# A stacked graph network on one core: the attention row s2 goes through memory, stored graph by graph and read back with step 1

## The reference, cut to what matters

```python
h = relu(layernorm(x))
for i in range(3):                        # the recurrent rounds
    aggr = einsum('bst,bsd->btd', adj != 0, h @ weight[i])
    h = gru_cell(aggr, h, w_ih, w_hh, b_ih, b_hh)     # gates r, z, n
x = x + h
h = relu(layernorm(x))
Wh = h @ W.T
s1, s2 = Wh @ a1, Wh @ a2                 # one value per node
e = leaky_relu(s1[:, :, None] + s2[:, None, :], 0.2)
att = softmax(where(adj == 0, -inf, e))
x = x + att @ Wh
```

## Time and profile before

| | before |
|---|---|
| time, median of 3 runs | 1824.64 us (1824.41 to 1824.9) |
| profiled execution | 1824.46 us, span 1822.6 us |
| PE busy | 1779.6 us (98%) |
| VectorE busy | 1417.3 us (78%) |
| ScalarE busy | 1022.5 us (56%) |
| POOL busy | 354.7 us (19%) |
| DMA, its queue's share | 30.0% of 16 engines |
| granted clock of TensorE, mean | 0.991 of full speed |

### The profile page before, as it was taken

The page is one execution under the profiler, slowest core; times in us unless marked ns, Lnnn a source line. Parts: engine busy times, 40 slices in busy tenths (PEclk is TensorE's granted clock), DMA queues, the critical chain, the costliest instruction groups (busy, mean ns, idle before and its releaser), DMA issues.

```text
span 1822.6 us, 32181 instructions
## 1 busy us (share of the span) xinstructions
PE 1779.6 (98%) x10492; PEld 945.1 (52%) x10492; DVE 1417.3 (78%) x2801; ACT 1022.5 (56%) x1822; POOL 354.7 (19%) x778
## 2 busy tenths in 40 slices
PE   6999999999999999999999999999999999999993
PEld 5444555545555454555545555454555545555552
DVE  6667788787887877788787887877788787887866
ACT  5556556555555555556555555555556555555552
POOL 1022130311303122130311303122130311303100
PEclk9999999999999999999999999999999999999997
DMA  3322332323323223322323324223322323323221
GB/s 104 76 64 65 70 75 58 90 66 69 87 40 104 57 59 91 69 75 58 89 66 68 87 39 105 57 60 90 69 75 58 88 67 68 88 39 88 41 69 41
DMA packets 325789, 128.87 MB, mean 71 GB/s; under 512 B 241280, under 2 KB 325760, under 8 KB 325760
## 3 DMA queue, kind: packets, MB, share of 16 engines
q1 hardware_dynamic: 325760, 128.50, 30.0%
HBM read 52.96 MB, written 16.78 MB: 38 GB/s over the span
## 4 chain that ended last, share of the span: by engine, by line
PE 96%; DVE 1%; issue 1%; ACT 0%; POOL 0%; DVEq 0%; POOLq 0%; ACTq 0%
PE z_bank L320 27%; PE r_bank L320 27%; PE hn_bank L320 14%; PE in_bank L320 14%; PE s_bank L320 3%; PE w_bank L320 3%; PE nb_bank L334 2%; PE nb_bank L335 2%; PE t_bank L762 2%; PE t_bank L776 1%; ACT relu_att L272 0%; DVE dot_terms L947 0%; PE nb_bank L320 0%; ACT u_hi L858 0%; DVE stats_att L250 0%
## 5 line engine op out<-in xcount | busy, mean ns | idle before, releaser
L837 ACT ACTIVATE n_out<-n_pre,bih 128x512 f32<-128x512 f32 x192 | 138.0, 719 | 238.9 <-DVE n_pre L901 238.6
L320 PE MATMUL hn_bank<-ht_s,wh_hi 128*128 128x512 f16 x768 | 228.4, 379 | 1.7 <-PEq L428 1.7
L846 ACT ACTIVATE ht_s<-ht 128x512 f16<-128x512 f32 x128 | 80.6, 630 | 264.5 <-DVE ht L917 264.5
L320 PE MATMUL r_bank<-ht_s,wh_hi 128*128 128x512 f16 x768 | 228.5, 379 | 0.0
L320 PE MATMUL z_bank<-ht_s,wh_hi 128*128 128x512 f16 x768 | 228.4, 379 | 0.0
L353 DVE TENSOR_TENSOR nb_lo<-nb_bank,nb_hi 128x512 f16<-128x512 f32 x192 | 131.1, 683 | 84.1 <-ACT nb_hi L349 84.0
L896 DVE SCALAR_TENSOR_TENSOR n_pre<-tanh_r,hn_b 128x512 f32<-128x512 f32 x192 | 146.3, 762 | 62.9 <-ACT tanh_r L832 59.0
L297 POOL TENSOR_TENSOR ln_gnn<-stats_gnn 128x4 f32<-128x4 f32 x32 | 18.6, 582 | 893.2 <-DVE stats_gnn L250 893.2
L832 ACT ACTIVATE tanh_r<-r_bank,b_rz,down 128x512 f32<-128x512 f32 x192 | 147.2, 767 | 65.9 <-PE r_bank L320 65.7
L827 ACT ACTIVATE hn_b<-hn_bank,b_hn,down 128x512 f32<-128x512 f32 x192 | 147.9, 770 | 57.0 <-PE hn_bank L320 57.0
L910 DVE SCALAR_TENSOR_TENSOR diff<-ht,n_out 128x512 f32<-128x512 f32 x192 | 132.0, 687 | 38.8 <-ACT n_out L837 38.5
(11 more groups left out here) (190 smaller groups left out, 3939.4 us busy)
## 6 DMA issues: line engine op xcount, KB each, us to landing
x_in<-in_x_dram SPq DMA_DIRECT2D x32, 512.0 KB, 3.8
x_res<-in_x_dram SPq DMA_DIRECT2D x32, 512.0 KB, 4.0
out_dram<-x_out SPq DMA_DIRECT2D x32, 512.0 KB, 5.2
adj_in<-in_adj_dram SPq DMA_DIRECT2D x32, 256.0 KB, 4.0
adj_att<-in_adj_dram SPq DMA_DIRECT2D x32, 256.0 KB, 4.3
h_s<-ht_s SPq DMA_TRANSPOSE x128, 3.0
ht_s<-h_s SPq DMA_TRANSPOSE x64, 3.2
raw_ih<-in_L_gnn_w_ih_dram SPq DMA_DIRECT2D x2, 384.0 KB, 3.7
```

Source lines behind the costliest of these rows:

```text
L320: last = nc.tensor.matmul(bank_ap, w, d, start=start and i == 0, stop=stop and i == len(todo) - 1)
L837: nc.scalar.activation(n_out[c][:], n_pre[c][:], ACT.Tanh, bias=bih[:, 4 + c:5 + c]).then_inc(n_ready, 1)
L846: nc.scalar.activation(ht_s[layer % 2][a][:, c, 0, :], ht[a][:, c, :], ACT.Copy, scale=HSCALE).then_inc(ht_hi_ready, 1)
```

## The change

For the groups whose attention runs beside gates (all but those of the last pair), `s2` no longer goes through TensorE. Two stages are new in the table, both on SP: `store_s2` waits for the dots and writes the 512 values to a tensor in device memory, `[GROUP, P]`, graph by graph, so that the four values of a partition go to four places 128 apart; `load_s2` waits until the store has landed, and until the sum of the group before has been made, and reads the 512 values as one row, with step 1, onto all 128 partitions of a new tile `s2_row`. VectorE waits for that load, and adds `s1` to `s2_row` instead of the bank. `s12` becomes two tiles, `s1` and `s2`. TensorE's part of `scores` returns at once except in the last pair, and `residual` loses its wait for the sum. The table places the even group's store in slot 1, step 1 and its load in slot 1, step 3, ahead of the sum in slot 1, step 6; the odd group's in slot 2, steps 5 and 7, ahead of slot 3, step 6.

```diff
@@ the table SIDE
-    (2, 5): [("neighbours", 1, 1, 1, 0)],
+    (2, 5): [("neighbours", 1, 1, 1, 0), ("store_s2", 1, -1)],
...
+    (1, 1): [("store_s2", 0, -1)],
+    (1, 3): [("load_s2", 0, -1)],
+    (2, 7): [("load_s2", 1, -1)],
@@ tiles
-        s12 = both("s12", [P, GROUP, 2], F32)
+        s1 = both("s1", [P, GROUP], F32)
+        s2 = both("s2", [P, GROUP], F32)
+        s2_row = sb("s2_row", [P, GROUP, P], F32)
+        s2_dram = [nc.dram_tensor(f"s2_dram{a}", [GROUP, P], F32, kind="Internal").ap() for a in range(2)]
@@ SP
+                def store_s2(p, a):
+                    if not after_gates(p):
+                        sp.wait_ge(dots_ready, per_group(p, a))
+                        with nc.allow_non_contiguous_dma(reason="512 values, graph by graph for the row"):
+                            sp.dma_start(s2_dram[a].rearrange("b t -> t b"), s2[a][:]).then_inc(s2_stored[a], 16)
+
+                def load_s2(p, a):
+                    if not after_gates(p):
+                        sp.wait_ge(s2_stored[a], per_load(p))
+                        wait_reached(sp, sum_ready, per_group(p, a) - 1)
+                        sp.dma_start(s2_row[:].rearrange("q b t -> q (b t)"),
+                                     s2_dram[a].rearrange("b t -> (b t)").unsqueeze(0).broadcast_to(
+                                         [P, T])).then_inc(s2_landed[a], 16)
@@ TensorE, residual and scores
-                    if a == 0 and c == 0:
-                        wait_reached(pe, sum_ready, per_group(p - 1, 1))
...
+                    if not after_gates(p):
+                        return
...
                         last = nc.tensor.transpose(scores_bank(p, a)[:, b * P:(b + 1) * P],
-                                                   s12[a][:, b, 1:2].broadcast_to([P, P]), ident[:])
+                                                   s2[a][:, b:b + 1].broadcast_to([P, P]), ident[:])
@@ VectorE, dots and scores
-                                                                  s12[a][:, b, i:i + 1])
+                                                                  (s1, s2)[i][a][:, b:b + 1])
...
-                    dve.wait_ge(s2_done, n)
+                    if after_gates(p):
+                        dve.wait_ge(s2_done, a + 1)
+                        row = scores_bank(p, a)[:].rearrange("p (b t) -> p b t", b=GROUP)
+                    else:
+                        dve.wait_ge(s2_landed[a], per_load(p))
+                        row = s2_row[:]
...
-                    nc.vector.tensor_tensor(score[:], scores_bank(p, a)[:].rearrange("p (b t) -> p b t", b=GROUP),
-                                            s12[a][:, :, 0:1].broadcast_to([P, GROUP, P]),
+                    nc.vector.tensor_tensor(score[:], row, s1[a][:].unsqueeze(2).broadcast_to([P, GROUP, P]),
```

More of the change, by code:

```diff
@@ L628, in scores_bank @@
         def scores_bank(p, a):
-            return (s_bank, hn_bank)[a] if after_gates(p) else t_bank
+            return (s_bank, hn_bank)[a]
         def gather_bank(p, half):
@@ L644, in graph_blocks @@
         pt_landed = [sem(f"pt_landed{a}") for a in range(2)]
+        s2_stored = [sem(f"s2_stored{a}") for a in range(2)]
+        s2_landed = [sem(f"s2_landed{a}") for a in range(2)]
         hn_ready, tanh_r_ready, n_ready, tanh_z_ready = (sem("hn_ready"), sem("tanh_r_ready"), sem("n_ready"),
@@ L715, in _ @@
                     "load_gnn": lambda p, a: load_gnn(sp, p, a), "store": store, "load_att": load_att,
[L716 removed]
+                    "probs_transpose": probs_transpose, "store_s2": store_s2, "load_s2": load_s2,
                     "transpose": transpose, "first_transpose": lambda *which: first_transpose_sp(sp, *which)})
@@ L765, in scores @@
                 def scores(p, a):
+                    if not after_gates(p):
+                        return
                     pe.wait_ge(dots_ready, per_group(p, a))
-                    if after_gates(p) and a == 1:
+                    if a == 1:
                         pe.wait_ge(hn_ready, per_gate(p, 1, LAYERS - 1, 1))
-                    elif after_gates(p):
+                    else:
                         pe.wait_ge(out_ready, per_chunk(p - 1, 1, 0))
[L771 to L774, removed]
                     for b in range(GROUP):
                         last = nc.tensor.transpose(scores_bank(p, a)[:, b * P:(b + 1) * P],
-                                                   s12[a][:, b, 1:2].broadcast_to([P, P]), ident[:])
+                                                   s2[a][:, b:b + 1].broadcast_to([P, P]), ident[:])
                     last.then_inc(s2_done, 1)
```

## The result

The changed kernel takes 1974.14 us (median of 6 runs) against 1824.77 for the kernel before (6 runs): ratio 1.083, 95% interval 1.0808 to 1.0853. It is slower by 149.4 us, where no measurable change was forecast. The row lands late: the rival that had a chance of 0.17, and far beyond the 1838 to 1862 that it was given.

A forecast was written before the change was run, and what follows sets the result against it. A loop of waits through VectorE, POOL and ScalarE, 109.38 us a pair, was taken to bound the kernel, not PE. The terms 0 - 0.44 + 0.3 - 1.4 + 0 = -1.5 took 1824.46 to 1823.0 us, range 1820.9 to 1826.

The forecast's parts named there:

- The row lands late: Rival, chance 0.17: store and load ahead of VectorE's sum exceed 8.0 us; 1838, 1853 or about 1862 us.
- The new wait: VectorE's wait for the row before the sum: store 3.7 us, load 3.05, landing 1.1 us early, cost 0.
- the 8.0 us: Time from the even group's store at about 1041.6 to the sum at 1049.58, within which store and load must land.
- The rival's price: Late row at VectorE's sum, chance 0.17: beyond 8.0 us, each us late is lost in each of 15 pairs.
- PE's transposes are worth nothing in the steady pairs: Removing 0.88 us of PE work a pair counts 0, since PE already waits in each; bounds 0 and -13.2.
- PE is the bound: Rival, chance 0.14: PE sets the pace, so removed transposes count, 13.2 us (1811.3) or 6.6 us (1817.9).
- The POOL step: POOL's small operations after stats_gnn: earlier PE gets POOL through 0.04 to 0.16 us earlier; 0.1 for 14 pairs, -1.4.
- the +0.3: VectorE's sum score reading memory instead of a bank: 692 ns instead of 683, 30 times, +0.3 us.
- PE's gap: PE's idle gap after the matmul at 1066.24, behind the previous tanh: to grow from 0.24 to about 1.1 us a pair.
- the same loop: Path of stalls through VectorE, POOL and ScalarE, 109.38 us a pair, that PE follows with 0.24 us to spare.

The follow-up runs named there:

- Spread out: The changed kernel with its 512 four-byte writes 512 B apart, the load reading x instead of s2: 1822.43 us, 0.9986 of the kernel before.
- the 8 B store: The changed kernel with its 512 four-byte writes 8 B apart, the load reading x instead of s2: 1843.74 us, 1.010 of the kernel before.
- the unheld store: The changed kernel with SP waiting for the store only a pair later and the load reading x at once: 1943.48 us, 1.0651 of the kernel before.
- the kernel with both quick halves: The changed kernel with s2 made a row in SBUF by four DMAs, stored to DRAM in one piece, then loaded: 1822.76 us, 0.9982 of the kernel before.

## Why the prediction was wrong

The step that failed is in "The new wait": *"A store of single values isn't in the trace ... From both sides: 2.3 and 5.2; I take 3.7."* It measured 9.8. The two bounds came from a load of single values and from a store of long rows. Neither writes many small pieces close together in DRAM, and that is where the price is: the same bytes cost 2.2 us spread out. A number between two unlike neighbours is no bound when the thing itself has a property that neither neighbour has.

The other end of the same sum was also off: the load took 4.9 rather than 3.05. Part of that has nothing to do with the slow store. The prediction counted the loads of `x_in` and `adj_in`, which SP issues between the store and the row's load of the even group, at 0.5 us of issuing. In *Spread out* the row's load takes 4.1 us in the even groups and 3.0 in the odd ones (medians of 15), which have no such loads in front; with the slow store it was 5.9 and 4.8. That these loads are the reason was not tested by itself. With a quick store the 8.0 us still hold it.

*The rival's price was too low although its mechanism was right.* It held 15 us for each us late, which the 8 B store confirms, and the 8.0 us available, measured at 7.97. With the landings measured it would have said 15 x 7.4 = 111, near the 114.8 that was waited. What it lacked is the rest: the DMAs behind the store. The prediction asked what SP holds up while it waits (the transpose of 1047.45 in the earlier trace rows) and stopped at "needs SP 2 us after the store should have landed", so it priced that at nothing. And a free SP would have given back only some 31 us, as the unheld store showed. I have not split the 149.4 into exact shares, since the waits overlap.

*The steps that held*, read in the kernel with both quick halves and in the spread store. PE's transposes are worth nothing in the steady pairs: the kernel with 30 x 4 fewer of them is 2.9 us faster in the profiled execution (1821.60 against 1824.46), not 6.6 or 13.2, so "PE is the bound" is out. The POOL step came as worked out. These are the rows of that kernel that answer to the earlier trace rows, on VectorE, POOL and ScalarE; its even sum starts 0.74 us earlier (1048.84 for 1049.58), so times are taken from the sum:

```profile
1098.22 0.69 DVE L923 SCALAR_TENSOR_TENSOR n_pre<-tanh_r,hn_b 128x512 f32<-128x512 f32 x1 [0.22 <-ACT tanh_r L859]
```

```profile
1098.45 0.53 POOL L310 TENSOR_TENSOR ln_gnn<-ln_gnn 128x4 f32<-128x4 f32 x1
1099.06 0.20 POOL L312 TENSOR_TENSOR ln_gnn<-ln_gnn,consts 128x4 f32<-128x4 f32 x1
```

```profile
1100.66 2.07 ACT L274 ACTIVATE relu_gnn<-x_in,ln_gnn 128x256 f32<-128x256 f32 x4 [2.52 <-POOL ln_gnn L316]
```

`n_pre` comes 49.38 us after the sum instead of 49.83, the 0.44 that PE had lost; POOL's held operation is now L310, which answers to L308 of the earlier trace rows, and the next (0.20, it was 0.69) runs free. `relu_gnn`, which waits for POOL, starts 51.82 us after the sum instead of 51.97, and a pair is 0.15 shorter, within the 0.04 to 0.16. Two small misses: the sum from memory stayed at 683 ns, so the +0.3 of the earlier trace rows did not come, and PE's gap did not grow where I said. PE in the same kernel:

```profile
1060.08 0.23 PE L336 MATMUL nb_bank<-adj_s,h_s 128*128 128x128 f16 x1 [0.43 <-DVE nb_lo L355]
...
1065.50 0.38 PE L322 MATMUL hn_bank<-ht_s,wh_lo 128*128 128x512 f16 x1
1065.86 0.60 PE L322 MATMUL r_bank<-ht_s,wh_hi 128*128 128x512 f16 x2
```

The place of the earlier trace rows has the same 0.36 between starts as before. The slack turns up ahead of `nb_bank`, where PE waits for VectorE. It is the same loop, met at an earlier hand-over. PE's busy time fell by 8.9 us, not by 13.

With a store that lands in 2 us the time is near the forecast of 1823.0: 1822.43 and 1822.76 were measured. That they meet so closely is in part luck: against the kernel before on the same chip these two are 2.8 and 2.9 us faster, where 1.5 was forecast.

## What to carry to other kernels

A transfer is priced by the shape of its writes, not by its bytes: 2 KB that are scattered as single values over neighbouring addresses in DRAM are dearer than 512 KB in rows (9.8 us against 5.2), and the DMAs issued behind them pay too, even from the other of the two queues tried. Turn a column into a row where small writes are quick (here SBUF) and write DRAM in whole pieces. And if a step has no row of its own kind in the trace, its upper bound is open: ask how late it may be before the critical loop notices (here 8.0 us) and whether the gain is worth that risk; here the gain was 3 us in 1825.

## What the runs showed of the hardware

- 512 four-byte writes to DRAM land in 2.2 to 2.3 us at 64 B apart or more, 3.1 at 16 B, 4.2 at 8 B and 9.8 at 4 B; the same bytes in pieces of 16 B, side by side, in 1.9. Into one SBUF partition, 4 B apart, 128 writes land in 2.0.
- The packets of such a store are no slower (9 ns at most); the time lies between the last of them and the landing.
- While such a store is under way, transfers of another queue and between other memories land late as well: up to 10.1 us for a transpose within SBUF (3.9 at most in the kernel before). Behind a slow load from one partition of SBUF, on the same queue, it is up to 12.1.
- A broadcast of 2 KB onto 128 partitions takes 3.3 us from DRAM and 11.7 from one partition of SBUF.
- An f32 operand read with step 4 makes the 128x512 sum 1098 ns instead of 683.
